# Top-32 attention of the convolution block, unrolled in units of four batches

## The reference

```
q = x @ Wq;  k = ctx @ Wk;  v = ctx @ Wv
s = (q_h . k_h) * 32**-0.5        for each head h, masked keys far below
keep the 32 largest of the 128 scores of each row and head
w = softmax over the kept ones
attn = mean over heads of w @ v, times gate and text mask
film_in, film_out = two scale and shift pairs from attn @ W_film, biases times gate
u = layernorm(x) * g_in + b_in,   then scaled and shifted by film_in
y = causal convolution of u over the tokens with the S4D kernel, plus u * D_skip
then film_out on y, the shortcut, a normalization, a feed-forward part
```

## Time and profile before

| what | value |
|---|---|
| median of 3 runs | 4036.98 us (4032.49 to 4044.03) |
| profiled execution | 4038.41 us, its span 4036.6 us |
| mean granted PE clock | 0.828 of full |
| busy over the span | PE 3061.0 us, VectorE 2229.9, ScalarE 1444.1, GpSimd 1388.7 |
| instructions | 85866 |
| HBM | 30.45 MB read, 2.23 MB written |

### The profile page before, as it was taken

One profiled execution on the slowest core, in us unless ns is written; L12 is line 12 of the kernel. 1 busy time (PEld: TensorE's weight loads), 2 busy tenths in 40 slices (PEclk: granted clock), 3 DMA queues, 4 the chain that ended last, 5 costly groups with the idle time before them and its releaser, 6 DMA issues. The chain is left out here.

```text
span 4036.6 us, 85866 instructions
## 1 busy us (share of the span) xinstructions
PE 3061.0 (76%) x32357; PEld 2179.3 (54%) x32357; DVE 2229.9 (55%) x6333; ACT 1444.1 (36%) x3558; POOL 1388.7 (34%) x2165
## 2 busy tenths in 40 slices
PE   6943555766556599899599977896548999987978
PEld 4522333644344377656489965564116666665657
DVE  6888999353445534466444444464445555544644
ACT  4522333153223455444322211453003333334544
POOL 3420111162222111244423332453453333324545
PEclk9975666685556799899699975897779999998979
DMA  2000000200000000000000000000000000000000
GB/s 85 3 7 2 0 0 0 83 9 5 0 0 0 27 1 2 33 3 3 1 6 1 1 6 0 8 2 35 0 0 5 2 2 2 2 2 7 2 1 21
DMA packets 24535, 37.17 MB, mean 9 GB/s; under 512 B 576, under 2 KB 21184, under 8 KB 23360
## 3 DMA queue, kind: packets, MB, share of 16 engines
q1 hardware_dynamic: 24224, 32.68, 2.5%
HBM read 30.45 MB, written 2.23 MB: 8 GB/s over the span
## 5 line engine op out<-in xcount | busy, mean ns | idle before, releaser
L1190 POOL TENSOR_TENSOR L_attn__qk<-L_attn__turned 128x512 f32<-128x512 f32 x128 | 161.4, 1272 | 381.2 <-DVE L_attn__turned L1299 381.2
L3706 PE MATMUL psum<-L_ffn_hT,weights 128*128 128x256 f32 x1024 | 245.1, 383 | 11.7 <-PEq L56 11.7
L774 DVE TENSOR_REDUCE L_xattn__nm<-psum 128x8 bf16<-128x1024 f32 x128 | 156.4, 1224 | 151.0 <-PE psum L967 144.9
L1299 DVE TENSOR_TENSOR L_attn__turned<-psum,weights 128x1024 f32<-128x1024 f32 x128 | 153.6, 1220 | 153.1 <-PE psum L1406 149.9
L3706 PEld LDWEIGHTS psum<-L_ffn_hT,weights 128*128 128x128 f32 x1024 | 187.0, 193 | 32.5 <-issue 11.8
L3645 DVE TENSOR_TENSOR L_ffn__e_a<-L_ffn__e_sg,psum 128x512 f32<-128x512 f32 x128 | 88.0, 687 | 187.8 <-ACT L_ffn__e_sg L3637 187.8
L3637 ACT ACTIVATE L_ffn__e_sg<-psum 128x512 f32<-128x512 f32 x128 | 76.4, 597 | 259.7 <-PE psum L3706 259.7
L714 ACT ACTIVATE L_xattn__pT<-psum 128x1024 f32<-128x1024 f32 x128 | 124.0, 1021 | 57.7 <-PE psum L995 57.7
L3717 PEld LDWEIGHTS psum<-weights,L_ffn__e_a 128*128 128x128 f32 x1024 | 134.4, 191 | 7.2 <-DVE L_ffn__e_a L3645 0.7
L1406 PE MATMUL psum<-L_attn__xT,weights 128*128 128x256 f32 x512 | 136.8, 401 | 1.7 <-DVE L_attn__turned L1299 1.0
L3717 PE MATMUL psum<-weights,L_ffn__e_a 128*128 128x128 f32 x1024 | 135.1, 275 | 0.5 <-DVE L_ffn__e_a L3645 0.5
(11 more groups left out here) (640 smaller groups left out, 8717.1 us busy)
## 6 DMA issues: line engine op xcount, KB each, us to landing
L_xattn__toeplitz<-s4d_kernel SPq DMA_DIRECT2D x8, 1024.0 KB, 5.5
weights<-pack SPq DMA_DIRECT2D x1, 3328.0 KB, 10.2
weights<-pack SPq DMA_DIRECT2D x1, 3140.0 KB, 10.6
weights<-pack SPq DMA_DIRECT2D x1, 2370.0 KB, 9.0
out_dram<-X SPq DMA_DIRECT2D x1, 2048.0 KB, 8.7
weights<-pack SPq DMA_DIRECT2D x1, 1732.5 KB, 10.3
ctxT<-ctxT_in SPq DMA_DIRECT2D x1, 1536.0 KB, 21.8
weights<-pack SPq DMA_DIRECT2D x1, 1376.0 KB, 5.7
```

The costliest lines, as they stand in the source:

```text
L774: nc.vector.tensor_reduce(nm[:, n % 2, :].rearrange("p (g c) -> p g c", g=4)[:, 2 * u:2 * u + 2, 0:4], scores[u].rearrange("p g (i q) -> p ...
L1190: nc.gpsimd.tensor_tensor(qk[:, p % 2, u], turned[:, g % 2, :, 0:2 * P], turned[:, g % 2, :, 2 * P:4 * P], ALU.add).then_inc(qk_sb, 1)
L1299: nc.vector.tensor_tensor(turned[:, g % 2], proj[u % 2].unsqueeze(1).to_broadcast([P, 2, 4 * P]), k.w(name + "rope").rearrange("p (t q) -> ...
L3706: last = nc.tensor.matmul(bank[g % 2][:, 256 * c:256 * c + 256], k.w(name + w)[:, o:o + P], hT, start=True, stop=True)
```

## The change

The top-32 block is written out without loops, in 8 units `u` of four batches `j`. The names of its tiles begin with `front_`.

- Scores: `key_bias` is now 8 rows of 512 columns, one row per unit, and a bf16 matmul with `head_row` adds it in PSUM. The scores of a head for four batches fill one bank (S[0] to S[3]); each is a matmul on 32 rows, without padding.
- VectorE keeps the four rounds (`best`, `replaced`), the first straight from PSUM. It also keeps the statistics, a shift for the normalization, the reciprocal and the product with `text_gate`.
- Selection: ScalarE takes exponentials of the scores (`ex`) and of what is left after four rounds (`exl`), where the chosen keys give zero. GpSimd subtracts the two; only the chosen keys remain.
- Weights: the reciprocal times gate is put on a diagonal (`diag`, GpSimd, per batch and head), and the matmul that turned the weights with the identity now multiplies with this diagonal.
- FiLM: bias rows are added by a bf16 matmul on three rows (`film_rows`, the bias split in three bf16 parts in the setup); ScalarE copies the result.
- Normalization: ScalarE does scale and shift, GpSimd gain, bias and input FiLM, on four batches at a time.
- The flips move into the block, one matmul per unit, and ScalarE copies the result into `UY`. They are gone from the convolution block.

The diff, cut to its core:

```diff
+            key_bias = hold("key_bias", [P, 4 * P], BF16)
+            film_rows = hold("film_rows", [3, 4 * DM], BF16)
-                        ts(key_bias[:], mask_keys[:], -NEG, NEG, ALU.mult, ALU.add)
+                        ts(key_bias[0:NB // 4, :], mask_keys[:], -NEG, NEG, ALU.mult, ALU.add)
+                        link(nc.vector.tensor_copy(part[0][:], fb))
+                        link(tt(over[0][:], fb, part[0][:], ALU.subtract))
+                        link(nc.vector.tensor_copy(part[1][:], over[0][:]))
...
+                        def chosen(u):
+                            pool.wait_ge(w_sb, u + 1)
+                            for j in range(4):
+                                i = 4 * u + j
+                                if i >= 2:
+                                    pool.wait_ge(am_ps, i - 1)
+                                nc.gpsimd.tensor_tensor(
+                                    diag[:, j % 2], k.w("ident").unsqueeze(1).to_broadcast([P, heads, P]),
+                                    den[:, 2, j, :].unsqueeze(2).to_broadcast([P, heads, P]),
+                                    ALU.mult).then_inc(diag_sb, 1)
+                                pool.wait_ge(exl_sb, i + 1)
+                                nc.gpsimd.tensor_tensor(ex[:, u % 2, j], ex[:, u % 2, j], exl[:, j % 2],
+                                                        ALU.subtract).then_inc(p_sb, 1)
...
+                        def rest(u):
+                            for j in range(4):
+                                i = 4 * u + j
+                                act.wait_ge(left_sb, 8 * u + 7 + j // 2)
+                                if i >= 2:
+                                    act.wait_ge(p_sb, i - 1)
...
+                        def filmed(u):
+                            act.wait_ge(v_ps, u + 1)
...
+                            for j in range(4):
+                                act.wait_ge(film_ps, 4 * u + j + 1)
+                                nc.scalar.activation(film[:, j, :], FB[:, 0:2 * DM], ACT.Copy)
+                                nc.scalar.activation(FO[:, 4 * u + j, :], FB[:, 2 * DM:4 * DM],
+                                                     ACT.Copy).then_inc(film_sb, 1)
...
+                        projected(0)
+                        for u in range(UNITS + 1):
+                            if u >= 1:
+                                denominators(u - 1)
+                            if u + 1 < UNITS:
+                                projected(u + 1)
+                            if u >= 1:
+                                rest(u - 1)
+                            if u < UNITS:
+                                exponentials(u)
+                                normed(u)
+                            if u >= 1:
+                                filmed(u - 1)
+                                flipped(u - 1)
...
-                                nc.vector.tensor_tensor(left[0][:, s], source[:, s], sc[:, s],
-                                                        ALU.not_equal).then_inc(sel_sb[s].sem, 1)
...
+                                if r == 0 and u >= 1:
+                                    inverse(u - 1)
...
+                        def film_of(u):
+                            pe.wait_ge(c_sb, u + 1)
+                            for j in range(4):
+                                if 4 * u + j >= 1:
+                                    pe.wait_ge(film_sb, 4 * u + j)
+                                nc.tensor.matmul(FB[:], ones_bf[0:3, :], film_rows[:], start=True, stop=False,
+                                                 skip_group_check=True)
+                                nc.tensor.matmul(FB[:], cT[:, j, :], k.w(name + "W_film"), start=False, stop=True,
+                                                 skip_group_check=True).then_inc(film_ps, 1)
```

More of the change, by code:

```diff
@@ L2417, in _ @@
                         nc.vector.memset(kz[:], 0.0)
+                        link(nc.vector.memset(key_bias[:], 0.0))
                         for i in range(2):
@@ L2518, in film_conv, with event @@
-                halves, moments, var_eps, rstd = (sig.pair(n) for n in ("halves", "moments", "var_eps", "rstd"))
-                lg_sb, ln_sb, u1_sb, u_sb = (sig.pair(n) for n in ("lg_sb", "ln_sb", "u1_sb", "u_sb"))
+                    return ctx.enter_context(nc.sbuf_tensor(f"{name}_front_{what}", shape, dt))
+                def event(what):
+                    return sig.one("front_" + what, 1, 1).sem
+                UNITS, K_TOP = NB // 4, 8 * rounds
+                xT, qT, kT = sb("xT", [P, 4 * P]), sb("qT", [P, 4 * P]), sb("kT", [P, 4 * P])
@@ L2716, in _ @@
+                        inverse(UNITS - 1)
+                        weights(UNITS - 1)
                     @block.tensor
                     def _(pe):
[L2718 to L2736 removed]
@@ new lines, in flip @@
+                        def flip(u):
+                            pe.wait_ge(u_sb, u + 1)
+                            nc.tensor.matmul(KV[:], k.w(name + "flip"), xg[:].rearrange("p j d -> p (j d)"), start=True,
+                                             stop=True).then_inc(flip_ps, 1)
+                        front(0)
+                        scores(0)
+                        for u in range(UNITS + 1):
+                            if u + 1 < UNITS:
+                                front(u + 1)
+                                if u == 0:
+                                    scores(1)
+                            if u >= 1:
+                                back(u - 1)
+                                if u + 1 < UNITS:
+                                    scores(u + 1)
+                                film_of(u - 1)
+                                flip(u - 1)
```

520 lines of the change are left out of this document (259 added, 261 removed).

## The result

| | before | after |
|---|---|---|
| median of 4 runs | 4036.77 us (4032.49 to 4044.03) | 3981.85 us (3973.84 to 3990.08) |
| ratio | | 0.9862, 95% interval 0.9837 to 0.9887 |
| profiled execution, span | 4038.41, 4036.6 us | 3983.9, 3982.1 us |
| VectorE, ScalarE, GpSimd busy | 2229.9, 1444.1, 1388.7 us | 2102.8, 1467.8, 1431.2 us |
| block's start to first convolution matmul | 426.4 us | 365.7 us |

A forecast was written before the change was run, and what follows sets the result against it. Bound: a chain through ScalarE's in-order queue, 42.3 us per unit against VectorE's 32. Block 31 + 8 × 42.3 = 369.4, plus 6.3 to the convolution: −50.7; setup +2.9; from 4038.4 to 3990.6, median 3989 us; range 3940 to 4027.

The forecast's parts named there:

- a: Start of each unit's chain: 16 denominators on ScalarE at 0.305 us each, 4.9 us.
- b: After the denominators: xT, Q, qT and kT, four exponentials, handovers; 5.0 us at 1.2 GHz (taken), 4.1 at 2.4.
- c: GpSimd up to its second difference, three operations of 1.27 us, awaited by the next exponentials: 3.8 us.
- d: ScalarE's remaining 20 exponentials, four normalizations, v, amT and handovers: 8.8 us, GpSimd's other four operations hidden inside.
- e: PE's context, mask and score matmuls, ahead of FiLM: 6.1 us at 1.2 GHz (taken), 3.3 at 2.4.
- f: FiLM of four batches in turn between PE and ScalarE, one bank: 12.8 us at 1.2 GHz, 8.4 at 2.4 (taken).
- g: Unit's end: two GpSimd operations, flip matmul, its copy, handovers; 5.3 us at 1.2 GHz (taken), 4.4 at 2.4.
- The ends: Block's ends: 35.6 us before the first denominators, first chain 6.5 longer, last two 4.5 and 6.5 shorter.
- The two times at one clock throughout: Whole kernel with PE all at 1.2 GHz, 4025 us (block 404.6), or all at 2.4, 3953 us (block 332.6).
- VectorE as the pace: Rival: in the top-32 block VectorE's 32 us per unit sets the pace; block 296, time 3915 us; chance 0.07.
- GpSimd as the bound: Rival: GpSimd operations in the block grow to 2.3 us (gain gone) or 2.5 (time 4065 us); chance 0.06.
- Clock low throughout: Rival: PE at 1.2 GHz throughout, another 1 us of handovers per unit, nothing measurable: 4026 to 4040 us; chance 0.09.

The follow-up runs named there:

- Experiment 2: Changed kernel with selection rounds 2 and 3 looking at and replacing only 16 of the 128 scores (32 largest not found): 3975.4 us, ratio to before 0.9827.
- experiment 1: Changed kernel with ScalarE copying the flip of a unit behind the next unit's denominators instead of in front: 3939.81 us, ratio to before 0.9748.
- experiment 5: Changed kernel with four buffers instead of two for the exponentials of what is left: 3964.16 us, ratio to before 0.981.
- experiment 3: Changed kernel with the flips put back in the convolution block: 3946.9 us, ratio to before 0.9767.
- 6: Changed kernel with the first two Toeplitz transfers issued during the top-32 block, into memory the stage doesn't use: 3974.12 us, ratio to before 0.9837.
- 7: Changed kernel with later flip copy, four buffers for exponentials of what is left, and first two Toeplitz transfers during the block: 3920.43 us, ratio to before 0.97.
- 9: Changed kernel with later flip copy, four exponential buffers, early Toeplitz transfers, and selection rounds 2 and 3 cut to 16 scores: 3915.35 us, ratio to before 0.9696.
- 10: Changed kernel with each diagonal made twice by GpSimd: 4019.56 us, ratio to before 0.9946.
- 8: Changed kernel with later flip copy, four exponential buffers, early Toeplitz transfers, and eight thrown-away matmuls per unit between K and Q: 3936.62 us, ratio to before 0.9738.
- experiment 4: Changed kernel with eight thrown-away bf16 matmuls of 512 columns between K and Q per unit, from the third on: 3964.83 us, ratio to before 0.9808.

## Why the prediction was right, point by point

The direction, the range and the mechanism were right; the time was 7 us too high (3989 against 3982). That is closer than the parts of the sum were, because two misses worked against each other: up to the convolution the forecast was 12.2 us too slow, behind that point 5.5 us too fast.

**The pace.** VectorE's work per unit, its wait in front of the reciprocal (61.3 us for seven, 5.7 to 9.2 each but for the last, a little under the 8 to 10 forecast) and the chain through ScalarE's queue are as told. Experiment 2 (VectorE's work goes, the unit stays) and experiment 1 (one place in the queue changes, 5 us per unit go) show it.

**The unit**, by the prediction's steps, in the unit from 494.04 to 534.26:

| step | forecast | measured | from, to |
|---|---|---|---|
| a denominators | 4.9 | 4.87 | 494.04, 498.91 |
| b xT, Q, first exponentials | 5.0 | 4.97 | 498.91, 503.88 |
| c to the second difference | 3.8 | 3.59 | 503.88, 507.47 |
| d ScalarE | 8.8 | 7.99 | 507.47, 515.46 |
| e context, masks, scores | 6.1 | 2.92 | 515.46, 518.38 |
| f FiLM | 8.4 | 10.48 | 518.38, 528.86 |
| g GpSimd, flip | 5.3 | 5.40 | 528.86, 534.26 |
| sum | 42.3 | 40.22 | |

The term that was most mis-sized is **e**. It was taken at 1.2 GHz, 6.1 us; the prediction names waits in front of b and g as the ground for the low clock there and gives none for e. In this unit it took 2.92, even under the other column's 3.3, with a granted clock of 1.00 from 515 on. Over the first six units it was 2.9 us three times and 4.5 three times. **f** was taken at 2.4 GHz throughout, 8.4 us; it was 8.7 to 8.8 in four of the six, and 10.5 (this unit) and 9.9 in the two in which the clock fell before its end. So the units differ by where in them the clock rises and falls: in those of 38.6 us (FiLM from 558.69 to 567.45 in one of them) both e and f are short, in those of 40.2 one of the two, in that of 41.4 neither. Where e was short, the last weighing had taken 1.7 to 2.0 us, so the clock had risen late; where it was long, the last two weighings had taken 1.13 each, which saved nothing, since they wait for GpSimd, and the clock had fallen again for context and scores. The granted clock was right in its mean and wrong in its place. **d** had the exponentials from PSUM at the price from SBUF; they took 4.21 us for 16 against 4.77 from SBUF in experiment 5, 0.035 less each, between the forecast's bounds of nothing and 0.13. **c** is smaller by the diagonal, 1041 ns instead of 1272.

**The ends.** The first reciprocal came 47.3 us after the start (35.6 + 4.9 + 6.5 = 47.0 forecast). The first six distances sum to 237.2 instead of 253.8. The last two units were to be 4.5 and 6.5 shorter, since they hold no next scores; they were not: the last distance was 41.1 instead of 37.8, and from the last reciprocal to the block's end 34.0 us passed instead of 30.8. In these two units, which have no projections and no scores for PE, the granted clock is 0.54, and 0.50 in the FiLM stretches; each batch of FiLM takes 3.4 us (two of the last unit's):

```profile
675.90 2.08 PE L2848 MATMUL psum<-weights,L_xattn__front_cT 128*128 128x512 f32 x2
...
679.32 2.08 PE L2848 MATMUL psum<-weights,L_xattn__front_cT 128*128 128x512 f32 x2
```
Together: +0.3 − 16.6 + 3.3 + 3.2 = −9.8, the block's 359.6 against 369.4. What the missing scores were to save at the end, the low clock took back in large part.

**Flips and transfer.** 6.2 us from the block's end to the first matmul, 6.3 forecast; experiments 3 and 6 show both sides of it. But the moved flips had a second price, which the prediction put at nothing ("No other part of the kernel changes"): the convolution's own 256 records took 52.44 us before and take 54.8 in the changed kernel and in every run with the flips in the block. With the flips back (experiment 3) they take 51.7. Before, the first 3.4 us of the convolution ran at a granted clock of 0.89, straight behind the flips; now, behind the wait, they run at 0.50. From there on it is 0.50 in both.

**Setup.** From SP's first issue of the stage (262.75 before, 261.62 after) to the last operation on the convolution kernel (331.50, 332.39) it grew from 68.75 to 70.77 us: +2.0 against +2.9. The eight operations took 4.7 us instead of 4.4; the key bias was as forecast. The wait for the mask (1.31 us) is gone, which the prediction named as possible and took for nothing.

**The sum.** The first convolution matmul was to come at 760.50 − 50.7 + 2.9 = 712.7 and came at 700.5, 12.2 earlier: 9.8 from the block, 2.3 because the block began earlier than forecast (0.9 from the setup, 1.1 because the stage before, which the change doesn't touch, ended earlier, 0.2 at the entry), 0.1 from the transfer. Behind it the profiled execution is 5.5 us longer than before (3281.6 against 3276.1). Of these, 2.4 are the convolution, as above. The other 3.1 lie in later stages, whose time differs by up to 9.6 us between the profiled executions, so nothing can be read from them. The two times at one clock throughout are each 1 us too high in the prediction: its own sum gives 4024 for all at 1.2 GHz and 3952 for all at 2.4.

**The rivals.** VectorE as the pace: refuted in the changed kernel (2); once the chain is cut it is level with ScalarE's queue (7 and 9). GpSimd as the bound: its operations do lie on the path when they are made longer (10), but in the changed kernel the eight took 1.04 and 1.27, nowhere over 2. Clock low throughout: refuted in the middle of the units, true at their flips and in the FiLM of the last two.

The Trainium skill ("TensorE: Matmul & The Clock Gate", on HAM oscillation) had been weighed there: it says that idle gaps between bursts send PE back to half clock, so that the next burst starts cold. This case's trace agrees for Q behind waits of 3.3 us and more (1.98 to 2.08 us) and for the flip behind 3.5 (2.07); the context behind a wait of 1.66 us ran at the high clock, but the gaps of the page's case are longer than that one. Taken for every burst of the chain, as in the prediction's upper column, the unit would have been 46.7 us, and none of the steady ones was over 41.4.

One link was not tested: no run moved the next scores behind FiLM in PE's order, so that step e holds FiLM back is read from the timeline alone.

## What to carry to other kernels

When work leaves the busy engine for others, write down every in-order queue of one iteration and look for the circle that closes through it (here: denominators, projections, exponentials, context, FiLM, flip, denominators); its sum is a floor of the new pace, even where no engine is over three quarters busy. A copy that waits for a long hand-over belongs behind the next iteration's first work, not ahead of it; the one here cost 38 us. Work that is moved out from beside a transfer lays the transfer open, and can change the clock of what follows. And cost PE's work in such a chain at both clocks, by its place in the unit: a microsecond taken out elsewhere can be worth two, and work added to hold the clock can lose it.

## What the runs showed of the hardware that was not expected

- MAX8 reads PSUM at the price of SBUF: 280 ns against 276 for 128 elements, MATCH_REPLACE8 281 against 274. An exponential of 128 columns is cheaper from PSUM, 4.21 us for 16 against 4.77 from SBUF (experiment 5).
- A GpSimd product of two broadcast operands took 1041 ns for 512 columns, less than the 1271 of a difference of two full ones. The prediction had feared the opposite.
- The granted clock answers to small shifts: 0.9 us saved ahead of FiLM made 2.6 of a unit (5), and with 1.7 us of extra matmuls ahead of Q the weighings and the context came at the low clock (8), while in experiment 4 the same matmuls brought Q to the high one. What decides between the two was not found.
- A PE without a gap is not always at the high clock: in the convolution before, from 767.3 to 812.9 us, PE is busy for 45.6 of 45.6 us by the profile, and the granted clock is 0.50 throughout.
- Sixteen score matmuls on 32 rows took 1.17 us together at the high clock, as 32 records; the forecast's 1.3 at that clock, taken from the row of 512 columns with four row groups, held for pieces of 128.
